# A transformer block on one core: when the second FFN's and the router's tokens are turned, and when the top two experts are picked

## The reference

```python
x = x + 0.5 * _L0_ffn_ref(_layernorm(x), ...)                    # a linear layer with a low-rank correction
x = x + _L0_attn_ref(_layernorm(x), ...)                         # 16 heads, two steps of softmax attention on unit keys
x = x + 0.5 * _L0_ffn_ref(_layernorm(x), ...)                    # the same linear layer again ("the second FFN")
x = x + 0.5 * _L1_ffn_ref(_layernorm(x), ...)                    # 8 experts, the top 2 of each token, and a shared one
x = x + _L1_attn_ref(_layernorm(x), ...)                         # 16 heads, a mask by blocks of 64
x = x + 0.5 * _L1_ffn_ref(_layernorm(x), ...)                    # the same experts again
```

```python
scores = jax.nn.softmax(xt @ gate_w.T, axis=1)
top_scores, sel = jax.lax.top_k(scores, TOP_K)      # TOP_K = 2
```

## Time and profile before

| | |
|---|---|
| runs | 3434.24, 3441.23, 3446.66 us; median 3441.23 |
| profiled execution | 3455.04 us, span from the first to the last instruction 3453.2 us |
| TensorE busy | 3178.5 us, 92% of the span |
| VectorE, ScalarE, GpSimd busy | 2358.3, 2077.4, 1267.3 us (68%, 60%, 37%) |
| mean granted TensorE clock | 0.976 of full speed |

### The profile page before, as it was taken

The page is one execution under the profiler, slowest core; times in us unless marked ns, Lnnn a source line. Parts: engine busy times, 40 slices in busy tenths (PEclk is TensorE's granted clock), DMA queues, the critical chain, the costliest instruction groups (busy, mean ns, idle before and its releaser), DMA issues.

```text
span 3453.2 us, 55298 instructions
## 1 busy us (share of the span) xinstructions
PE 3178.5 (92%) x19942; PEld 1655.9 (48%) x19942; DVE 2358.3 (68%) x5153; ACT 2077.4 (60%) x2689; POOL 1267.3 (37%) x2419
## 2 busy tenths in 40 slices
PE   5898998999999999999999999999999999998899
PEld 2444544444544444454444445444444544444557
DVE  1646575867678676767867676786867677676573
ACT  2464566666656666665666666666666656665442
POOL 3224232342535334243533424353343435223321
PEclk8899999999999999999999999999999999999999
DMA  1000100010110100111010011101101111000110
GB/s 42 1 32 3 33 1 8 28 32 35 32 35 29 32 17 23 35 32 35 29 32 16 24 35 32 35 30 32 35 5 35 32 35 31 30 32 4 60 35 35
DMA packets 81502, 96.89 MB, mean 28 GB/s; under 512 B 50544, under 2 KB 68400, under 8 KB 81104
## 3 DMA queue, kind: packets, MB, share of 16 engines
q1 hardware_dynamic: 81232, 93.35, 8.4%
HBM read 82.76 MB, written 4.78 MB: 25 GB/s over the span
## 4 chain that ended last, share of the span: by engine, by line
PE 61%; ACT 15%; DVE 14%; POOL 5%; issue 4%; SPq 0%; DMA 0%; ACTq 0%; DVEq 0%; POOLq 0%
PE ps L689 16%; PE ps L706 14%; ACT probs L820 13%; PE ps L771 8%; PE ps L761 8%; DVE negmax L1072 6%; PE ps L589 5%; PE ps L726 4%; PE ps L595 2%; PE ps L584 2%; PE ps L654 1%; DVE hid L1141 1%; DVE uts L1039 1%; DVE th L1135 1%; DVE X L951 1%
## 5 line engine op out<-in xcount | busy, mean ns | idle before, releaser
L820 ACT ACTIVATE probs<-ps 128x1024 f32<-128x1024 f32 x1536 | 1573.6, 1024 | 1009.3 <-PE ps L689 994.3
L1072 DVE TENSOR_REDUCE negmax<-ps 128x2 f32<-128x1024 f32 x1024 | 1250.3, 1221 | 450.9 <-PE ps L726 432.8
L689 PE MATMUL ps<-qT,kT 32*128 32x512 f32 x3072 | 778.8, 502 | 116.7 <-ACT probs L820 68.7
L706 PE MATMUL ps<-probs,v 128*32 128x512 f32 x6144 | 838.5, 618 | 0.0
L1310 POOL TENSOR_TENSOR xe<-xT_m,G 128x512 f32<-128x512 f32 x288 | 367.7, 1278 | 990.7 <-PE ps L761 945.1
L761 PE MATMUL ps<-xe,w_sb 128*128 128x256 f32 x2304 | 655.3, 409 | 13.2 <-DVE hid L1141 8.9
L689 PEld LDWEIGHTS ps<-qT,kT 32*128 32x128 f32 x3072 | 289.0, 184 | 766.9 <-ACT probs L820 506.0
L726 PE MATMUL ps<-kT,qT 32*128 32x512 f32 x2048 | 520.5, 503 | 57.2 <-DVE negmax L1072 56.5
L761 PEld LDWEIGHTS ps<-xe,w_sb 128*128 128x128 f32 x2304 | 399.2, 192 | 185.5 <-issue 132.6
L1135 DVE SCALAR_TENSOR_TENSOR th<-th,ps 128x256 f32<-128x256 f32 x576 | 236.3, 411 | 187.5 <-ACT th L850 182.2
L850 ACT ACTIVATE th<-ps 128x256 f32<-128x256 f32 x576 | 221.0, 384 | 151.0 <-PE ps L761 138.5
(11 more groups left out here) (171 smaller groups left out, 2687.7 us busy)
## 6 DMA issues: line engine op xcount, KB each, us to landing
G<-gates_dram SPq DMA_DIRECT2D x96, 768.0 KB, 6.3
maxrow<-negmaxT SPq DMA_DIRECT2D x512, 2.0 KB
v<-v_tok SPq DMA_DIRECT2D x256, 18.0 KB, 1.9
X<-in_x SPq DMA_DIRECT2D x16, 256.0 KB, 2.8
out<-X SPq DMA_DIRECT2D x16, 256.0 KB, 2.3
w_sb<-in_w SPq DMA_DIRECT2D x1, 1152.0 KB, 7.4
w_sb<-in_w SPq DMA_DIRECT2D x1, 576.0 KB, 8.5
gates_dram<-gT SPq DMA_DIRECT2D x32, 18.0 KB
```

Source lines behind the costliest of these rows:

```text
L689: nc.tensor.matmul(ps[:, B_ST + h, :], kT[a][rows, g * S + kc * P:g * S + (kc + 1) * P], qT[a][rows, g * S:(g + 1) * S], start=True, stop= ...
L706: ins = nc.tensor.matmul(ps[ROWS * j:ROWS * (j + 1), B_UT, :], v[:, at:at + ROWS], probs[:, n % QUADS, j, :], start=(kc == 0), stop=(kc == ...
L820: nc.scalar.activation(probs[:, quad % QUADS, j:j + 2, :], ps[:, B_ST:B_ST + 2, :], ACT.Exp).then_inc(sem["exp_done"], 1)
L1072: nc.vector.tensor_reduce(negative[:, tc, 2 * half:2 * half + 2], ps[:, B_SM:B_SM + 2, :], AX_X, ALU.max, negate=True).then_inc(sem["sm_re ...
```

## The change

Three things. In `ffn_events` and `moe_events` the gap between the sums and the turning grows from 0.2 to 1.2 slots (for `ffn_xt` only in the second FFN, k=1). And `m_index` is no longer placed where it first fits: in a slot in which some job has an `sm`, it has to wait until two slots after it could first have been placed; in a slot without any it is placed 0.3 into the slot at the earliest.

```diff
+RESTED = {"m_index": 2}
+REST_FROM = 0.3
...
+        reduced = {int(pos // 1) for pos, _, name, _ in self.marks if name == "sm"}
...
+        arrived = {}
...
                 pos = max(pos, placed[other] + gap)
+            if name in RESTED:
+                if slot in reduced and slot < arrived.setdefault(key, pos) + RESTED[name]:
+                    return None
+                if slot not in reduced:
+                    pos = max(pos, slot + REST_FROM)
...
-    t.at(start + 1.4, "ffn_xt", b, k, behind=(("ffn_stats", b, k), 0.2))
+    t.at(start + 1.4, "ffn_xt", b, k, behind=(("ffn_stats", b, k), 1.2 if k else 0.2))
...
-    t.at(start + 1.4, "m_xt", b, k, behind=(("m_stats", b, k), 0.2))
+    t.at(start + 1.4, "m_xt", b, k, behind=(("m_stats", b, k), 1.2))
```

## The result

| | before | changed |
|---|---|---|
| median (lowest to highest) | 3440.0 us (3434.24 to 3448.86), 6 runs | 3476.03 us (3467.11 to 3482.74), 6 runs |
| ratio, 95% interval | | 1.0092 (1.0074 to 1.0111) |
| profiled execution, span, mean clock | 3455.04, 3453.2, 0.976 | 3476.91, 3475.1, 0.973 |

The changed kernel is slower by 0.9%, some 32 us, where 3443 was forecast with a range up to 3464. The prediction is wrong.

What follows compares the result with a forecast made beforehand. TensorE, busy 92% of the span, was taken as the bound, with its waits. The terms -20.4 - 1.4 + 26.4 + 0.5 - 9.7 + 5.8 = +1.2 us on 3441.2 gave 3443, range 3422 to 3464.

Steps and rivals of the forecast that it cites:

- first and second place, images 3 to 14: Turning and top two of k=0: 1.7 us sooner in each of 12 turns, 20.4 us in all.
- the same, images 1 and 2: Turning and top two of k=0 in turns without the 1.45 us wait: 0.7 us sooner each, 1.4 in all.
- falls around slot 21 vanish: Clock falls there in five of twelve turns end as waits for VectorE shorten: 5 x 1.9 = 9.7 us sooner.
- falls at slots 72 and 79: New wait of 2 us at slot 79 brings the clock down in three of twelve turns: 5.8 us later.
- First place: The turning for k=0: of TensorE's 1.45 us wait about 0.6 arrives, since TensorE then waits for VectorE instead.
- Second place: The top two of k=0: following 2.9 slots later, they make the `sm` 1.1 us sooner per turn.
- VectorE gives nothing back: Rival: at the top two of k=0 only 0.6 of the 1.7 us arrives, 13 us more, 3456; chance 0.16.
- Third place: Gates of k=1: turned 2.4 us later, delaying G and the maxima behind it; 2.2 us in 12 images, 26.4 later.
- the maxima don't wait for G: Rival: GpSimd's addition of maxima stays put, k=1's gates cost only 0.4 us a turn, 3415; chance 0.12.
- half is swallowed: Rival: half the lateness at k=1's gates goes into existing waits on VectorE and for `stack0q`, 3430; chance 0.14.
- The clock: Granted TensorE clock: 9.7 us sooner from falls ending around slot 21, 5.8 later from new ones at slot 79.
- The step from profile to median: The profiled execution's 13.8 us above the median was carried over: 3441.2 + 1.2, rounded to 3443.

Runs made afterwards that it cites:

- pool_back: The changed kernel with `p0_res` placed 1.4 slots later in GpSimd's order, so the picking of k=1 stands ahead of it again; 3450.61 us, ratio 1.0014.
- sp_rows_first: The changed kernel with SyncE's `m_gt` 0.6 slots later, so four `maxrow` DMAs go ahead of the gates and G; 3431.04 us, 0.9962 without one outlier.
- fill_pause: The changed kernel with `m_index` delayed only at k=0, plus four identity products in TensorE's pause at slot 17; 3421.29 us, ratio 0.9949 to the kernel before.
- gaps_only: The changed kernel without its second part: longer gaps kept, top two placed as before; 3441.87 us, ratio 0.9994 to the kernel before.
- rest_k0: The changed kernel with the short gaps of 0.2 and `m_index` delayed only at k=0; 3418.27 us, ratio 0.9938 to the kernel before.
- rest_k0_sp: Short gaps, `m_index` delayed only at k=0, and on SyncE the maxima DMAs ahead of k=1's gates; 3404.29 us, ratio 0.9893 to the kernel before.

## Why the prediction was wrong

The steps of the prediction against the profiled executions (us, all turns):

| step | forecast | measured |
|---|---|---|
| first and second place, images 3 to 14 | -20.4 | -20.4 |
| the same, images 1 and 2 | -1.4 | about -2.5 |
| third place without the clock | +26.9 | about +40 |
| falls around slot 21 vanish | -9.7 | -9.7 |
| falls at slots 17 to 20 | 0 | +16 |
| falls at slots 72 and 79 | +5.8 | +9 |
| start, tail, slots 11 to 14 | 0 | -8 |
| sum | +1.2 | +21.9 |

(The measured rows are from my stretches and rounded; they add up to 24.4. Of the difference 2.1 is a fall before in slots 14 to 17 of one turn, which is in no row.)

- **First place, right.** 14 to 17 gives 1.76, 17 to 20 takes 1.17: 0.6 a turn arrives, as walked.
- **Second place, right.** 20 to 24 gives 1.91, 24 to 30 takes 0.80: 1.1 a turn. The rival that VectorE gives nothing back falls.
- **Third place: the path right, its size wrong, and this is the first step that failed (13 us).** "TensorE has the gates at 1087.25 now; ... 2.2 us later", "0.2 us of waiting on each", 2.2 a turn in the end. Measured are 3.66 for the gates and 3.5 a turn. `pool_back` gives 2.5 and 2.3, as the walk had. The other 1.2 is VectorE's picking, 1.55 us longer beside `p0_res`. The prediction saw that `p0_res` begins "in the 2.05 us that it idles ahead of the picking now", and took this as cover; it priced the two engines as if neither could hold up the other. The rivals that the maxima don't wait for G, and that half is swallowed, both fall: `sp_rows_first` takes away what the first says isn't there. The rule of the Trainium skill that the first leant on ("DMA: Bandwidth & Descriptors", section "Queues, rings and completion order") doesn't free these maxima: added 7.5 us behind their issue with G ahead, and 3.3 with the order exchanged.
- **The clock: the second step that failed, and the larger (16 us for the new falls, 3 for those at slots 72 and 79).** "If it doesn't fall there any more: 5 x 1.9 = 9.7 us sooner" was true of slot 21, and new falls came at slot 17, in 7 turns at 2 to 3.8 us there, less 0.6 in the slots behind. The prediction foresaw the pause (the first place: "TensorE waits for VectorE instead") and didn't ask what the clock does behind it. It argued against falls behind a single wait from the 1.45 of the earlier trace rows, and that observation was true and didn't carry over: behind this one of 0.88 the clock fell in about half of the turns. `fill_pause`, where it never fell there, shows that this pause has to do with it.
- **The step from profile to median.** The profiled execution of before, 3455.04, lies above all of its timed runs. "3441.2 + 1.2" carried that distance of 13.8 over unchanged; the profiled execution of the changed kernel stands 0.9 above its median. So of the 33 us that the median lies above the forecast, 21.9 - 1.2 = 20.7 are the walk's and some 12 are this step's (the sum gave 3442.4, put down as 3443). In the twelve runs of `gaps_only` the slowest, 3454 us, has the lowest mean clock, 0.968, and the fastest, 3433 us, the highest, 0.981: such distances go with falls of the clock, and before's profile (0.976) had a lower clock than its usual run (0.979 to 0.982 as the mean of each later comparison). A credit for "vanishing" falls that are counted in one such execution is too high for the median.

Also wrong was the use of a range: with 12 turns, 1 us in a turn is 12 us. The prediction says so itself and then gives third place 2.8 as its upper bound, from waits for banks alone.

## What to carry to other kernels

When a change moves a long instruction of GpSimd beside short ones of VectorE of the forms seen here, price the short ones as blocked until the long one ends, before calling the idle time cover. Where a wait is moved, ask what TensorE's clock did behind such a pause, and count falls over several executions rather than one. And look at what stands behind large transfers in a DMA queue: putting four small DMAs ahead of three of 768 KB gained 0.5% by itself, nearly what the change's best part gave (`rest_k0`, 0.6%), and the two added up (`rest_k0_sp`, 1.1%).

## What the runs showed of the hardware

- Short VectorE instructions (128x32) beside a GpSimd instruction of 1.0 to 1.3 us end with it: 0.17 to 0.63, 0.29 to 1.38 us, in all 12 turns. Of eight 128x8 ones with one SBUF tensor the first does, and the eight go from 1.16 to 2.24.
- Behind one pause of 0.88 us the granted clock fell to its lower level in 41 turns of 84 (seven kernels, 3 to 7 of 12 in each), beginning 0.2 to 2.3 us after its end, at a net 1.4 to 3.2 us each in the changed kernel; with the pause filled, in none of 12. Behind another of 1.45 us it fell in 3 of 60. Eight 128x128 passes behind the pause held nothing up, and ran in 2.08 us in place of 1.16 while it was low.
- What four DMAs of 2 KB brought, issued behind three of 768 KB, was used 7.6 and 7.5 us behind their issue, by an engine that waited for it; with nothing ahead of them 3.4 us, and with the order exchanged 3.3.
